# Gathers and scatters of the dense pass issued in groups of four, each group behind TensorE's next tick

## The chip, the cores and the metric

One NeuronCore of one Trainium2 chip runs the whole program. The time is the device time of one execution in microseconds (us), smaller is better. Engines are called as in the profile: PE (TensorE), DVE (VectorE), ACT (ScalarE), POOL (GpSimd) and SP (SyncE, which only issues DMAs here).

## What is computed

Four graph layers in a row on one graph of 50,000 nodes with 128 features and 25,000 edges (edges sorted by destination). Each is `x = layernorm(x + layer(x))`:

```python
# 1: two GIN convolutions and a linear layer
agg = segment_sum(x[src], dst, N); h = relu((x + agg) @ wa + ba) @ wb + bb      # per convolution
# 2: relational convolution, 8 relations, weights from 4 bases
agg = segment_sum(x[src] * edge_weight, type * N + dst); out = einsum('rni,rio->no', agg, W)
# 3: normalised graph convolution
out = segment_sum(norm * (x @ W.T)[row], col) + bias
# 4: three attention layers (softmax over the edges of a destination), each with a layer norm
```

At least half of the nodes have no incoming edge, so most of the work on the nodes needs no neighbours.

## The kernel before

Nodes are worked on as if they had no neighbours in a **dense pass** (`dense_part`), and the rows of destinations are recomputed edge by edge afterwards. The program has these stages, one behind the other: a start (weights, index columns), the dense pass together with the first edge pass of GIN (`phase_dense_gin1`), the second GIN pass, the relational pass, the normalised pass, and the three attention layers.

**Dense pass.** `DG` = 98 ticks, one per group of 512 nodes. In each tick PE, ACT, DVE and SP run stages of up to nine successive groups, tied to one another by semaphores: PE's product L856 with its semaphore `pe_a`, ACT's `de_ha` (L911), PE's L844, ACT's `de_ht` (L890), PE's transposes L849, PE's L838, ACT's `de_hh`, PE's L828 in two halves, DVE's `de_r` (L955) and the norms, PE's transposes L862 and its product L1732. A full tick has 44 matmul records on PE (a float32 matmul has two records), and the first ticks, in which the late stages have not begun, have 32. ACT's instruction at L911 runs once per tick, so its starts give the length of each tick. SP issues the loads and stores of a tick, and in the first `COPIES` = 28 ticks also one piece of 903 KB of a copy of x into the table `t_xw` (L799).

**POOL in the dense pass** runs a program of its own, `slot_gathers`, whose instructions are indirect DMAs of 128 rows each. The order is written out by hand:

- 140 gathers of destination rows of x into `msgs` (`resident_gather`, L684); 24 others went ahead in the start
- a wait until the 28 pieces of the copy have landed (`x_copied`, L705)
- 197 scatters of slot numbers, 4 bytes per row, into a column of `t_xw` (L707)
- the last 33 destination gathers (L684)
- a wait for all scatters (`mapped`), and then the gathers of source rows into a ring (L700): 16 of them at once, and each four more behind PE's and DVE's progress in the edge pass

Before the change nothing ties POOL's 370 operations to the ticks. PE waits in the first edge pass for all destination rows (`got`, L1100).

**Later edge passes** use `gather_group` (L670): four gathers per tick, with a wait for a free place in a ring of four groups ahead of each four. In the relational pass ACT's L1652 runs once per tick, in the normalised pass ACT's L1863.

Of the kernel before, what the change touches and what calls it, by code (L numbers as in the profile page):

```python
# [23 lines left out]
D = 128  # L24
# [4 lines left out]
CHUNKS = 2 * ROWP  # L29
USED = -(-E // CE)  # L30
# [3 lines left out]
DG = -(-N // GN)  # L34
# [3 lines left out]
COPIES = 28  # L38
# [4 lines left out]
UN = 4  # L43
FIRST = 24
EVERY = 5
NR = 3
XR = 6
L = 3
# [72 lines left out]
def wait(eng, sem, value):  # L121

    if not isinstance(value, int) or value > 0:
        eng.wait_ge(sem, value)
# [31 lines left out]
class Net:  # L156
# [531 lines left out]
    def slot_gathers(self, pool, ring, sem, arrived, turned, taken):  # L688


        nc, a = self.nc, self.a
        mapped = sem("g_mapped")

        def rows(i):
            u = i % UN
            if i >= UN:
                pool.wait_ge(turned, i - UN + 1)
                pool.wait_ge(taken, i - UN + 1)
            for j in self.filled(i):
                nc.gpsimd.indirect_dma_start(  # L700
                    out=ring[:, u, j, :], out_offset=None, in_=self.xw,
                    in_offset=bass.IndirectOffsetOnAxis(ap=self.src_i[:, i * G4 + j:i * G4 + j + 1], axis=0)).then_inc(arrived[u], 16)

        self.resident_gather(self.dst_i, a["x"], D, self.got, range(FIRST, FIRST + EVERY * COPIES))
        pool.wait_ge(self.x_copied, 16 * COPIES)  # L705
        for c in range(USED):
            nc.gpsimd.indirect_dma_start(  # L707
                out=self.places, out_offset=bass.IndirectOffsetOnAxis(ap=self.put_i[:, c:c + 1], axis=0),
                in_=self.slot_id[:, c:c + 1], in_offset=None).then_inc(mapped, 16)
        self.resident_gather(self.dst_i, a["x"], D, self.got, range(FIRST + EVERY * COPIES, CHUNKS))  # L710
        pool.wait_ge(mapped, 16 * USED)
        for i in range(AG):
            rows(i)
# [40 lines left out]
    def dense_part(self, block, sem, pool_program):  # L754


        nc, a = self.nc, self.a
        mem, sb, ps = self.part("de")
        with mem:
            x = sb("x", [128, UN, G4, D])  # L760
# [17 lines left out]
            s = {n: sem(n) for n in names}  # L778
            last_rows = (N - (DG - 1) * GN) // G4
            self.dense_stores = out2, out3, outx, outh  # L780

            @block.sync
            def _(sp):
# [1139 lines left out]
    def phase_gats(self):  # L1923
# [5 lines left out]
        with ctx:  # L1929
            nh = sb("nh", [128, NR, G4, XW]); nnt = sb("nnt", [D, 2, GN]); nsq = sb("nsq", [D, 2, GN])  # L1930
            nsd = sb("nsd", [128, 2, G4]); ninv = sb("ninv", [128, 2, G4])
            ah = sb("ah", [128, NR, G4, XW]); fl = sb("fl", [128, UN, GN], BF16)
            tt = sb("tt", [D, 2, GN]); ant = sb("ant", [D, 2, GN]); asq = sb("asq", [D, 2, GN])
# [10 lines left out]
            p_nh = ps("p_nh", (128, 2, 512)); p_ah = ps("p_ah", (128, 2, 512))  # L1944
            narr = [sem(f"narr{u}") for u in range(NR)]; aarr = [sem(f"aarr{u}") for u in range(NR)]; farr = [sem(f"farr{u}") for u in range(UN)]
            nout = [sem(f"nout{u}") for u in range(3)]; aout = [sem(f"aout{u}") for u in range(3)]
# [65 lines left out]
            def _(sp):  # L2012
                def nodes(i):
                    if i < NODES:
                        layer, g = divmod(i, DG)
                        wait(sp, pe_nt, i - NR + 1)
                        if layer > 0:
                            sp.wait_ge(nout[(i - DG) % 3], 16 * ((i - DG) // 3 + 1))
                        sp.dma_start(nh[:, i % NR], self.nodes(self.th[layer], 0, g)).then_inc(narr[i % NR], 16)
                    if FIRST2 <= i - 1 < NODES:  # L2020
# [14 lines left out]
                def load(layer, g):  # L2035
                    s = layer * AG + g
                    wait(sp, dve_aw, s - NR + 1)
                    if layer > 0:
# [594 lines left out]
```

## Time and profile before

| what | us |
|---|---|
| median of 3 runs | 4961.03 (4953.85 to 4983.9) |
| profiled execution | 4922.33 |
| its span | 4920.6 |

The profile covers one execution. In it the dense pass runs from about 54 us to 1185 us of the span, and the first edge pass begins its gathers again at 1232 us. Over the whole span PE is busy 62%, DVE 54%, ACT 46% and POOL 39%. Times of rows are us from the span's start; "idle before" is the time that the engine stood still ahead of a row.

### The profile page before, as it was taken

Reading aid. Unit: us, or ns where it says so; the run is one execution under the profiler, and the core shown is the slowest. Engines: PE = TensorE matmul, PEld = TensorE weight load, DVE = VectorE, ACT = ScalarE, POOL = GpSimd, SP = SyncE. Lnnn points to the kernel's source line nnn. Section 1 sums busy time; section 2 is a strip of 40 time slices with the busy share of each in tenths; the row PEclk is TensorE's granted clock in tenths of the full one; section 3 lists DMA queues with packets and bytes.
Section 4 is the critical chain, followed back from the end, with each engine's and each line's share of the span. In section 5 each row is a group of like instructions: output and inputs, shape, how many; then the busy total and the mean of one; then the engine's idle time right before and its main releaser. Section 6 shows DMA issues by size and latency. Waiting matters only on the chain. (4 is left out here: it accounts for less than half of the span.)

```text
span 4920.6 us, 67479 instructions
## 1 busy us (share of the span) xinstructions
PE 3040.0 (62%) x18099; PEld 2447.4 (50%) x18099; DVE 2637.4 (54%) x8154; ACT 2245.0 (46%) x5893; POOL 1923.9 (39%) x1994
## 2 busy tenths in 40 slices
PE   1183008997887787785664039991089991058675
PEld 1062006775443454443563039990079881057665
DVE  2083008998444565796562017770047881068876
ACT  0072008886111344675453027770057770057765
POOL 6605760000553563663664730007700007700465
PEclk8596559998776787997776569895588875586655
DMA  3293016665554343454663237772256763255443
GB/s 116 69 333 115 12 38 210 222 223 178 149 154 124 88 117 112 127 172 146 177 202 121 63 102 244 219 225 63 59 183 205 226 197 84 66 171 196 142 133 96
DMA packets 419338, 723.50 MB, mean 147 GB/s; under 512 B 76431, under 2 KB 137908, under 8 KB 418606
## 3 DMA queue, kind: packets, MB, share of 16 engines
q1 hardware_dynamic: 350990, 610.53, 38.1%
q0 software_dynamic: 63040, 107.35, 8.7%
q10 hardware_dynamic: 5024, 2.30, 0.2%
q8 instruction: 122, 2.00, 0.2%
q14 instruction: 162, 1.33, 0.1%
HBM read 428.65 MB, written 321.10 MB: 152 GB/s over the span
## 5 line engine op out<-in xcount | busy, mean ns | idle before, releaser
L684 POOL DMA_INDIRECT msgs<-t_gat,row_i x591 | 566.9, 959 | 1149.7 <-DMA t_gat<-t_hn 923.1
L1739 PE MATMUL t_p_q<-mean_col,t_nsq 128*128 128x1 f32 x2352 | 341.5, 266 | 288.7 <-issue 248.0
L1739 PEld LDWEIGHTS t_p_q<-mean_col,t_nsq 128*128 128x128 f32 x2352 | 350.7, 228 | 301.1 <-issue 301.1
L2246 ACT ACTIVATE t_nnt<-t_p_nt,cxt 128x512 f32<-128x512 f32 x294 | 200.6, 682 | 592.8 <-remote 356.8
L700 POOL DMA_INDIRECT dg_g_ring<-t_xw,src_i x197 | 189.4, 961 | 648.2 <-DVE slot_id L1203 572.6
L2083 PE MATMUL t_p_nt<-ident,t_nh 128*128 128x128 f32 x1176 | 219.5, 318 | 264.7 <-issue 179.2
L1732 PE MATMUL t_p_nh<-wx,t_nnt 128*128 128x132 f32 x1568 | 258.0, 314 | 185.8 <-issue 127.3
L2006 POOL DMA_INDIRECT out_rows<-t_hn,own_i x197 | 201.2, 1021 | 401.9 <-issue 335.3
L1732 PEld LDWEIGHTS t_p_nh<-wx,t_nnt 128*128 128x128 f32 x1568 | 222.1, 216 | 186.7 <-issue 186.1
L2083 PEld LDWEIGHTS t_p_nt<-ident,t_nh 128*128 128x128 f32 x1176 | 160.0, 164 | 280.6 <-issue 261.9
L828 PE MATMUL de_p_o<-wc,de_hh 128*128 128x128 f32 x1568 | 219.3, 284 | 112.1 <-DVE de_r L955 86.6
L1753 DVE TENSOR_TENSOR t_hn<-t_p_nh,t_ninv 128x264 f32<-128x264 f32 x392 | 151.2, 427 | 251.1 <-remote 170.1
L707 POOL DMA_INDIRECT t_xw<-slot_id,put_i x197 | 191.2, 971 | 228.2 <-DMA t_xw<-in_x_map 165.8
L828 PEld LDWEIGHTS de_p_o<-wc,de_hh 128*128 128x128 f32 x1568 | 200.8, 198 | 132.2 <-issue 113.1
L2390 DVE RECIPROCAL t_ninv<-t_nsd 128x4 f32<-128x4 f32 x196 | 34.6, 176 | 430.4 <-issue 267.3
L676 POOL DMA_INDIRECT g_ring<-t_h,row_i x197 | 193.1, 980 | 178.2 <-PE g_p_t L1344 57.0
L1732 PE MATMUL de_p_h<-wx,de_x3t 128*128 128x132 f32 x784 | 121.2, 300 | 226.5 <-issue 166.5
L676 POOL DMA_INDIRECT gc_ring<-t_x,row_i x197 | 193.3, 981 | 151.4 <-POOLq L182 57.4
L676 POOL DMA_INDIRECT rg_ring<-t_x,row_i x197 | 192.7, 978 | 149.0 <-issue 52.7
L881 ACT ACTIVATE de_hh<-de_p_c,b2a 128x512 f32<-128x512 f32 x196 | 134.9, 688 | 221.3 <-remote 217.0
L1564 PE MATMUL rg_p_b<-bases,rg_gt 128*128 128x512 f32 x400 | 205.4, 618 | 31.8 <-DVE rg_mg L1682 22.4
L1732 PEld LDWEIGHTS de_p_h<-wx,de_x3t 128*128 128x128 f32 x784 | 101.2, 199 | 248.7 <-issue 169.9
(411 smaller groups left out, 8704.4 us busy)
## 6 DMA issues: line engine op xcount, KB each, us to landing
t_gat<-t_hn SPq DMA_DIRECT2D x296, 264.0 KB
t_nh<-t_gat SPq DMA_DIRECT2D x294, 264.0 KB
t_x<-de_x SPq DMA_DIRECT2D x196, 256.0 KB
t_ah<-t_gat SPq DMA_DIRECT2D x150, 264.0 KB
t_gat<-de_h SPq DMA_DIRECT2D x98, 264.0 KB
t_xw<-in_x_map SPq DMA_DIRECT2D x28, 903.0 KB
de_xt<-in_x_t SPq DMA_DIRECT2D x98, 256.0 KB
t_xn<-t_x SPq DMA_DIRECT2D x98, 256.0 KB
```

The source lines that it names most:

```text
L676: self.nc.gpsimd.indirect_dma_start(out=ring[:, u, j, 0:width], out_offset=None, in_=table, in_offset=bass.IndirectOffsetOnAxis(ap=idx[:, ...
L684: self.nc.gpsimd.indirect_dma_start(out=self.msgs[:, c, 0:width], out_offset=None, in_=table, in_offset=bass.IndirectOffsetOnAxis(ap=idx[: ...
L700: nc.gpsimd.indirect_dma_start(out=ring[:, u, j, :], out_offset=None, in_=self.xw, in_offset=bass.IndirectOffsetOnAxis(ap=self.src_i[:, i ...
L707: nc.gpsimd.indirect_dma_start(out=self.places, out_offset=bass.IndirectOffsetOnAxis(ap=self.put_i[:, c:c + 1], axis=0), in_=self.slot_id[ ...
L828: m = nc.tensor.matmul(p_o[:, j * D:(j + 1) * D], hh[:, u % 2, t, j * D:(j + 1) * D], self.wc[:, t, :], start=(t == 0), stop=(t == 1))
L1564: nc.tensor.matmul(p_b[j][:], gt[:, (u - 1) % 2, j * D:(j + 1) * D], self.bases[:].rearrange("i b o -> i (b o)"), start=True, stop=True).t ...
L1732: last = self.nc.tensor.matmul(p_h[:, j // 2, (j % 2) * XW:(j % 2 + 1) * XW], xt[:, j * D:(j + 1) * D], self.wx[:, layer, :], start=True, ...
L1739: last = self.nc.tensor.matmul(p_q[:, j:j + 1], sq[:, j * D:(j + 1) * D], self.mean_col[:], start=True, stop=True)
L1753: last = self.nc.vector.tensor_tensor(rows[:, 2 * b:2 * b + 2, :], t, self.over(inv[:, 2 * b:2 * b + 2], XW), ALU.mult)
L2006: nc.gpsimd.indirect_dma_start(out=self.out, out_offset=bass.IndirectOffsetOnAxis(ap=self.own_i[:, c:c + 1], axis=0), in_=held[:, g % XR, ...
L2083: t = nc.tensor.transpose(p_nt[:, j * D:(j + 1) * D], nh[:, g % NR, j, 0:D], self.ident[:])
L2246: nc.scalar.activation(nnt[:, g % 2], p_nt[:], ACT.Identity, bias=bias).then_inc(act_nt, 1)
```

## The change

`slot_gathers` counts the indirect DMAs that it has issued in the dense pass. Ahead of each four (`PACE`) it waits until PE's semaphore `pe_a` has reached the number of groups issued so far plus one, so that group n goes out in tick n. The same operations are issued in the same order; the other engines' programs are not touched.

```diff
+PACE = 4
...
+        begun = self.dense_begun
+        done = [0]
+
+        def after_ticks(ops):
+            wait(pool, begun, min(done[0] // PACE + 1, DG))
+            done[0] += ops
+
+        def targets(chunks):
+            for c in range(chunks.start, min(chunks.stop, USED), PACE):
+                group = range(c, min(c + PACE, chunks.stop, USED))
+                after_ticks(len(group))
+                self.resident_gather(self.dst_i, a["x"], D, self.got, group)
...
-        self.resident_gather(self.dst_i, a["x"], D, self.got, range(FIRST, FIRST + EVERY * COPIES))
+        targets(range(FIRST, FIRST + EVERY * COPIES))
         pool.wait_ge(self.x_copied, 16 * COPIES)
         for c in range(USED):
+            if c % PACE == 0:
+                after_ticks(min(PACE, USED - c))
             nc.gpsimd.indirect_dma_start(
...
-        self.resident_gather(self.dst_i, a["x"], D, self.got, range(FIRST + EVERY * COPIES, CHUNKS))
+        targets(range(FIRST + EVERY * COPIES, CHUNKS))
...
+            self.dense_begun = s["pe_a"]
```

POOL's instructions from the start of the dense pass to the first source gathers, before:

```order
31 L813 MEMSET de_x 128x2048
32 L684 DMA msgs<-in_x,dst_i 128x128 x140
33 L707 DMA t_xw<-slot_id,put_i 6498304x1 [waits x_copied]
34 L707 DMA t_xw<-slot_id,put_i 6498304x1 x196
35 L684 DMA msgs<-in_x,dst_i 128x128 x33
36 L700 DMA dg_g_ring<-t_xw,src_i 128x129 [waits dg_g_mapped]
37 L700 DMA dg_g_ring<-t_xw,src_i 128x129 x15
```

The same place of the change, first at the step from gathers to scatters (a semaphore is printed by the first name that its number had, so `st_dst_row` stands for `pe_a`):

```order
100 L685 DMA msgs<-in_x,dst_i 128x128 [waits st_dst_row]
101 L685 DMA msgs<-in_x,dst_i 128x128 x3
102 L722 DMA t_xw<-slot_id,put_i 6498304x1 [waits st_dst_row,x_copied]
103 L722 DMA t_xw<-slot_id,put_i 6498304x1 x3
104 L722 DMA t_xw<-slot_id,put_i 6498304x1 [waits st_dst_row]
```

And at the end of the paced part:

```order
215 L685 DMA msgs<-in_x,dst_i 128x128 [waits st_dst_row]
216 L685 DMA msgs<-in_x,dst_i 128x128 x3
217 L685 DMA msgs<-in_x,dst_i 128x128 [waits st_dst_row]
218 L713 DMA dg_g_ring<-t_xw,src_i 128x129 [waits dg_g_mapped]
219 L713 DMA dg_g_ring<-t_xw,src_i 128x129 x15
```

What were three runs of 140, 197 and 33 operations with one wait among them are now 94 groups of four or fewer (35, 50 and 9), each with a wait; the last one waits for tick 93 of 98, and the sixteen source gathers follow it in one piece as they did before.

## Rows read from the trace of the kernel before

**Rows 1.** Windows: time; busy us (records) of PE, PEld, DVE, ACT, POOL; clock, DMA share, GB/s.
```profile
67.00:253.00 186.00, 24.60 (x96) 16.71 (x96) 8.79 (x35) 9.54 (x19) 123.74 (x131) 0.55 0.25 83
276.00:399.00 123.00, 111.41 (x835) 87.46 (x835) 114.09 (x455) 104.74 (x265) 0.00 (x0) 1.00 0.98 358
399.00:745.00 346.00, 39.04 (x188) 27.49 (x186) 24.41 (x99) 22.98 (x59) 240.82 (x246) 0.54 0.10 27
745.00:1168.00 423.00, 382.85 (x2854) 299.15 (x2855) 392.58 (x1562) 360.18 (x912) 0.00 (x0) 1.00 0.64 223
```

**Rows 2.** Timeline of ACT, its L911: start, us, then the instruction; once per dense tick.
```profile
66.69 0.47 ACT L911 ACTIVATE de_ha<-de_p_a,b1a 128x256 f32<-128x256 f32 x1 [1.08 <-issue]
...
252.72 0.47 ACT L911 ACTIVATE de_ha<-de_p_a,b1a 128x256 f32<-128x256 f32 x1
...
399.27 0.47 ACT L911 ACTIVATE de_ha<-de_p_a,b1a 128x256 f32<-128x256 f32 x1
...
431.12 0.47 ACT L911 ACTIVATE de_ha<-de_p_a,b1a 128x256 f32<-128x256 f32 x1 [7.47 <-issue]
...
554.32 0.47 ACT L911 ACTIVATE de_ha<-de_p_a,b1a 128x256 f32<-128x256 f32 x1 [11.73 <-remote]
...
677.52 0.47 ACT L911 ACTIVATE de_ha<-de_p_a,b1a 128x256 f32<-128x256 f32 x1 [11.74 <-remote]
...
744.97 0.46 ACT L911 ACTIVATE de_ha<-de_p_a,b1a 128x256 f32<-128x256 f32 x1
...
1174.19 0.47 ACT L911 ACTIVATE de_ha<-de_p_a,b1a 128x256 f32<-128x256 f32 x1
```

**Rows 3.** Timeline of PE in one of the long ticks.
```profile
587.35 2.05 PE L828 MATMUL de_p_o<-wc,de_hh 128*128 128x128 f32 x8 [18.91 <-DVE de_r L955]
615.13 0.66 PE L849 MATMUL de_p_b<-ident,de_ht 128*128 128x128 f32 x2 [25.73 <-issue]
```

**Rows 4.** POOL's scatters by their source line: ns min/median/max, first and last start.
```profile
L707 POOL DMA_INDIRECT t_xw<-slot_id,put_i x197: 965/970/1198, 399.4 to 652.0; - x197
```

**Rows 5.** Timeline of POOL: a destination gather, and the last source gather ahead of its pause.
```profile
231.37 0.95 POOL L684 DMA_INDIRECT msgs<-in_x,dst_i  x1 [0.30 <-issue]
...
717.00 1.09 POOL L700 DMA_INDIRECT dg_g_ring<-t_xw,src_i  x1 [0.30 <-issue]
```

**Rows 6.** Windows of the relational pass, with and without POOL's gathers.
```profile
2067.00:2097.00 30.00, 26.25 (x101) 14.71 (x100) 28.14 (x91) 23.81 (x86) 19.05 (x20) 1.00 0.62 177
2251.00:2263.00 12.00, 10.70 (x42) 6.07 (x42) 11.53 (x38) 9.79 (x36) 0.00 (x0) 1.00 0.43 136
```

**Rows 7.** ACT's L1652, once per tick of the relational pass, in the same two windows.
```profile
2067.72 0.57 ACT L1652 ACTIVATE rg_gt<-rg_p_t 128x512 f32<-128x512 f32 x1
...
2085.70 0.57 ACT L1652 ACTIVATE rg_gt<-rg_p_t 128x512 f32<-128x512 f32 x1
...
2251.75 0.57 ACT L1652 ACTIVATE rg_gt<-rg_p_t 128x512 f32<-128x512 f32 x1
...
2263.53 0.57 ACT L1652 ACTIVATE rg_gt<-rg_p_t 128x512 f32<-128x512 f32 x1
```

**Rows 8.** Normalised pass, ACT's L1863 per tick: four ticks with gathers, one without.
```profile
2406.39 0.60 ACT L1863 ACTIVATE gc_x3t<-gc_p_x 128x512 f32<-128x512 f32 x1
...
2429.98 0.58 ACT L1863 ACTIVATE gc_x3t<-gc_p_x 128x512 f32<-128x512 f32 x1
...
2615.27 0.58 ACT L1863 ACTIVATE gc_x3t<-gc_p_x 128x512 f32<-128x512 f32 x1
2619.29 0.58 ACT L1863 ACTIVATE gc_x3t<-gc_p_x 128x512 f32<-128x512 f32 x1
```

**Rows 9.** ACT's L1652 around the 28 gathers that open the relational pass.
```profile
1968.11 0.60 ACT L1652 ACTIVATE rg_gt<-rg_p_t 128x512 f32<-128x512 f32 x1
1989.83 0.57 ACT L1652 ACTIVATE rg_gt<-rg_p_t 128x512 f32<-128x512 f32 x1
```

## The prediction

> **What bounds the kernel now.** I began with the page's slices, in which PE, DVE and ACT nearly stop in two stretches of the dense pass while POOL is busy, and cut the dense pass along them [rows 1]. From 276 to 399 us, and again from 745 to 1168, POOL does nothing and PE has 6.8 records per us at full clock. From 67 to 253 and from 399 to 745 POOL issues one indirect DMA after another, and PE has 96 records in 186 us and 188 in 346 us, about 0.5 per us. It is not the DMA engines that are full: in the second such stretch they are busy 10% of the time, against 98% in the fast stretch from 276 to 399.
>
> The ticks give the price [rows 2]. From 744.97 to 1174.19 there are 66 ticks in 429.22 us, 6.50 each. From 554.32 to 677.52 one tick takes 123.20 us. The stall is in PE: its L828 has 8 records that seem to be through at 589.4 us, but the next work of PE, L849, stands until 615.13 behind 25.73 us of "issue" [rows 3]. What PE waits for there is ACT, which had itself waited for PE's earlier product; the records' ends are modelled, so PE has really not been through. 123.20 us over the 44 records of a tick is 2.80 us per record, whatever its size. POOL meanwhile issues a gather each 0.95 + 0.30 = 1.25 us and a scatter each 1.27 us [rows 4, 5], without a break. So a long unbroken run of indirect DMAs on POOL goes together with a PE that needs 2.80 us per record, and everything else in the tick hangs on PE. I can't say from the trace what PE waits for.
>
> What is lost: from 66.69 to 252.72 there are three ticks (96 records of 32 each) in 186.03 us, and from 399.27 to 744.97 four ticks in 345.70 us [rows 1, 2]. Seven ticks at 6.50 are 45.5 us; 186.03 + 345.70 - 45.5 = **486 us** lost. Since the whole program runs one stage behind the other, a dense pass that ends earlier moves everything behind it.
>
> **The change part by part.**
>
> *Removed: the long runs.* 370 operations in unbroken runs of 140 and 230 become groups of four, one per tick. If PE stays fast, a tick is 6.50 us and a group takes 4 x 1.25 = 5.0 us, at most 5.1 with scatters [rows 4, 5], so POOL keeps up and pauses at least 1.4 us per tick. Gain: 486 us, less the following.
>
> *What a group of four costs PE.* The dense pass has no such row; the nearest is the relational pass, with exactly this pattern: 20 gathers in 30 us, four per tick, at full clock [rows 6]. Its tick is (2085.70 - 2067.72) / 3 = 5.99 us with gathers and (2263.53 - 2251.75) / 2 = 5.89 without [rows 7]. That is 0.10 us per tick, with a pause of only 1 us. The lower bound is nothing: nothing in the groups helps PE. The upper bound is the normalised pass: (2429.98 - 2406.39) / 4 = 5.90 us with gathers and 4.02 without, 1.88 us more [rows 8]. Of this 0.98 is simply that four gathers take 5.0 us, which doesn't bind in a tick of 6.50; the other 0.90 could be PE's delay. The dense pass lies nearer the relational pass in its length and in the pause; but it has 44 small records with several round trips between PE and ACT in a tick, where the relational pass has 20 records and a PE that is nearly always busy. I take 0.25 us, and keep 0 and 0.9. For 65 ticks behind the copy 0.25 x 65 = 16 us.
>
> *Gathers beside the copy of x.* In the first 28 ticks the DMA engines are already busy 98% and move 358 GB/s, 2.33 MB per tick [rows 1]. Before, POOL's gathers ran there mostly while the copy crawled with the ticks. Now each of these ticks has four gathers of 128 x 512 bytes more, 0.26 MB or 11%. If the engines can't move more, a tick grows by 0.11 x 6.50 = 0.7 us; if their share has slack, by as much as any tick. I take 0.5 x 28 = 14 us (ends: 0 and 28 x 1.6 = 45, both causes at their worst).
>
> *The waits added.* POOL waits 94 times for PE's `pe_a`. Queued behind each are only POOL's own gathers and scatters. Nobody waits for these within the dense pass. The wait for `x_copied` doesn't bind any longer: the copy's last piece goes out in tick 28, and POOL gets there in tick 36. The last group goes out in tick 93, so all destination rows are there before tick 98 ends, when PE wants them. If that cover were gone (more groups than ticks), each group over would cost 5 us.
>
> *The sixteen source gathers.* They follow the last group without a break: 17 operations, 21 us, in ticks 93 to 97. The nearest row is the run of 28 gathers which opens the relational pass: the tick in it takes 1989.83 - 1968.11 = 21.72 us instead of 5.89, 16 us too many [rows 9]. This run is shorter; I take 10 us and keep 0 and 24 (up to 16, and half as much again for a tick behind it). Before, these sixteen ended at 718.1 and the tick was free again only at 744.97 [rows 2, 5], which is inside the 486.
>
> *Sum.* 486 - 16 - 14 - 10 = 446 us. Against the profiled execution 4922.3 - 446 = 4476; its time lies 38.7 under the median of the runs shown, and the same saving from the median is 4961.0 - 446 = **4515 us**. With each term at its best, 486, it is 4475; with each at its worst, 486 - 0.9 x 65 - 45 - 24 = 358, it is 4603.
>
> **The rivals.**
>
> *Partial: PE stays slow for part of every tick.* Each group of four finds 3 or 4 round trips between PE and ACT, and a delay of 2.80 us in one or two of them lengthens the tick by 2.8 to 4. For it: the normalised pass has a surplus that may be this [rows 8]. Against it: the relational pass [rows 7]. At 3 us for each of 93 ticks, 279 - 30 (what the sum has for the ticks already) = about 250 us of the gain are gone: about 4765.
>
> *No change: the cost goes by the operation.* If each indirect DMA costs PE a fixed time, 486 / 370 = 1.31 us, then spreading them out moves the cost but saves nothing: ticks of 6.5 + 5.2 = 11.7 us, the end at about 4960. For it: POOL's runs and the slow ticks coincide exactly. Against it: four gathers would cost the relational tick 5.2 us and cost it 0.10 [rows 7].
> The same time is what a rule of the Trainium skill asks for, on another mechanism: in "SBUF — State Buffer", section "SBUF: two separate sides", PE never waits for another engine's port, and DMAs and compute instructions don't slow one another. By that rule POOL's gathers are not what holds PE, and to space them out would do nothing, 4961 again. The trace speaks against the rule taken this widely: PE has 0.5 records per us beside an unbroken POOL and 6.8 without, with the DMA engines at 10% and 98%.
>
> *Slower: each group leaves PE slow beyond its own end.* After POOL's last operation at 718.1 us the next tick begins only at 744.97, 27 us later [rows 2, 5]. If a group of four already brought PE into that state, each of 94 ticks would carry such a tail. At 27 us that is 94 x 27 - 486 = 2050 us more, about 7000. It decides from 486 / 94 = 5.2 us per group on. Against it: the relational pass and, less so, the normalised one run hundreds of gathers in fours without it [rows 7, 8]. For it: only that the dense pass has shorter records and more of them.
>
> **How the numbers follow.** The forecast, with PE fast in nearly every tick: 0.86. Partial: 0.06. No change: 0.04 (0.02 by a price per operation, 0.02 by the rule of the skill's page). Slower: 0.04. The range reaches from just under the best case, 4470, to a little over the worst of the forecast's own terms, 4640, because the price of a group in a tick with many round trips is the least known of them. A change of 1% is about what a measurement of this kernel can tell from none: faster by more 0.92, within it 0.04, slower 0.04.
>
> **What would show each step.** ACT's L911 should come each 6.5 to 7.5 us from tick 3 to 93, with none over 12 us in between; ticks 4 to 28 should be somewhat longer than the later ones, with the DMA share near 1. POOL should show four operations, then an idle time of 1 us or more that ends with PE. The dense pass should end near 740 us and the source gathers begin again near 790 instead of 1232. Ticks 94 to 98 should hold one or two of 10 to 25 us. Everything behind the first edge pass should have its old length. Wrong would be: ticks near 12 us throughout (a price per operation), ticks over 12 us with PE idle behind "issue" (slow state in groups of four), or a first edge pass that begins late because POOL's last groups or its sixteen source gathers are late.

## The result, and the profile after

| | before | changed |
|---|---|---|
| median | 4972.47 us (4 runs, 4953.85 to 4987.73) | 4661.26 us (4 runs, 4620.23 to 4692.79) |
| profiled execution, its span | 4922.33, 4920.6 us | 4656.54, 4654.8 us |
| ratio of the times, 95% interval | | 0.9348 [0.9271, 0.9425] |

The change saves 311 us between the medians; the ratio leaves out the changed kernel's run of 4692.79 us, which counts as slow, being over 1.5% above the fastest. The forecast was 446, and the measured time lies 21 us above the range: the direction and the mechanism of the stall held, and one term of the sum was nine times too small.

Two of the page's rows of 40 slices, first of the kernel before, then of the changed one with its span. The two holes at the left of PE's row (dense pass) are gone, and POOL's work is spread.

```profile
PE   1183008997887787785664039991089991058675
...
POOL 6605760000553563663664730007700007700465
```

```profile
span 4654.8 us, 67480 instructions
...
PE   4877777578869968846630399930499850178665
...
POOL 5544444155365546536657300067200037400555
```

Windows of the changed kernel, in columns as in [rows 1]: the first 28 ticks (28 intervals, from the start of tick 0 to that of tick 28), the ticks with groups behind them, the last five intervals.

```profile
60.00:256.00 196.00, 161.03 (x1131) 121.04 (x1132) 149.92 (x602) 139.37 (x347) 112.50 (x113) 0.97 0.97 351
262.00:819.00 557.00, 413.35 (x2772) 313.02 (x2770) 381.76 (x1513) 350.55 (x883) 257.39 (x255) 0.93 0.52 171
819.00:873.00 54.00, 33.41 (x230) 26.55 (x229) 30.28 (x122) 28.47 (x73) 16.30 (x17) 0.81 0.44 147
```

In [rows 1] PE had 0.5 records per us while POOL worked and 6.8 while it did not. Now it has 2772 / 557 = 5.0 with POOL at work in every tick. ACT's line L911 is now L927; its starts, as in [rows 2] (tick 0, 11, 28, 36, 86, 92, 93, 94, 97):

```profile
59.83 0.47 ACT L927 ACTIVATE de_ha<-de_p_a,b1a 128x256 f32<-128x256 f32 x1 [4.26 <-PE de_p_a L872]
...
129.56 0.47 ACT L927 ACTIVATE de_ha<-de_p_a,b1a 128x256 f32<-128x256 f32 x1
...
255.73 0.47 ACT L927 ACTIVATE de_ha<-de_p_a,b1a 128x256 f32<-128x256 f32 x1
...
329.50 0.46 ACT L927 ACTIVATE de_ha<-de_p_a,b1a 128x256 f32<-128x256 f32 x1
...
768.09 0.47 ACT L927 ACTIVATE de_ha<-de_p_a,b1a 128x256 f32<-128x256 f32 x1
...
819.46 0.47 ACT L927 ACTIVATE de_ha<-de_p_a,b1a 128x256 f32<-128x256 f32 x1
844.39 0.46 ACT L927 ACTIVATE de_ha<-de_p_a,b1a 128x256 f32<-128x256 f32 x1
853.39 0.46 ACT L927 ACTIVATE de_ha<-de_p_a,b1a 128x256 f32<-128x256 f32 x1
...
872.68 0.47 ACT L927 ACTIVATE de_ha<-de_p_a,b1a 128x256 f32<-128x256 f32 x1
```

The first 28 intervals take (255.73 - 59.83) / 28 = 7.00 us each, in two parts: (129.56 - 59.83) / 11 = 6.34, then (255.73 - 129.56) / 17 = 7.42. The 50 from tick 36 to 86 take (768.09 - 329.50) / 50 = **8.77** each, where a tick without POOL takes 6.50. I use these 50 ticks as the measure for every kernel below: there each tick holds one group of four. The tick from 819.46 takes 24.93 us and the next 9.00. The last tick begins at 872.68 instead of 1174.19, 301.5 us earlier. Behind it the changed kernel takes 3782.1 us to the end of the span, the one before 3746.4.

Where a tick grew is seen in its inner order. PE, POOL and ACT of the changed kernel in one tick of 8.2 us (L860 was L844 before, L865 was L849, L906 was L890):

```profile
426.54 0.59 PE L860 MATMUL de_p_b<-de_ha,w1b 128*128 128x256 f32 x2
427.32 1.16 PE L844 MATMUL de_p_o<-wc,de_hh 128*128 128x128 f32 x8 [0.18 <-DVE de_r L971]
429.70 0.38 PE L865 MATMUL de_p_b<-ident,de_ht 128*128 128x128 f32 x2 [1.22 <-issue]
...
423.71 0.96 POOL L722 DMA_INDIRECT t_xw<-slot_id,put_i  x1 [3.03 <-PE de_p_a L872]
424.98 1.24 POOL L722 DMA_INDIRECT t_xw<-slot_id,put_i  x1 [0.30 <-issue]
...
427.80 1.04 POOL L722 DMA_INDIRECT t_xw<-slot_id,put_i  x1 [0.30 <-issue]
...
428.93 0.47 ACT L906 ACTIVATE de_ht<-de_p_b,b1b 128x256 f32<-128x256 f32 x1 [2.09 <-issue]
```

PE's L860 seems to be through at 427.13, but ACT's L906, which needs its product and nothing else at that point, begins at 428.93, after an idle time of 2.09 us, and PE then stands 1.22 us for ACT. That is [rows 3] in small: the record's modelled end is early, and the product is really there later, while POOL's four DMAs are going out. POOL's program has 3 us to spare behind PE's L872, so it is not short of time.

But the place where `de_ht` begins is telling: POOL's fourth DMA ends at 427.80 + 1.04 = 428.84, and ACT's L906 begins at 428.93. In ticks 36 to 85 of the changed kernel this is so in 46 of 50: `de_ht` begins only when the fourth DMA of the group has ended (within 0.15 us in 23, 0.6 to 1.25 us behind it in 22), although no semaphore ties it to POOL. So by the program nobody waits for POOL's groups, and yet PE's product reaches ACT only with their end.

### The profile page after: what moved, and what is told of

Its sections match the earlier page's. It is cut to its first block and busy times, and to the rows that moved or that the text cites. A ratio compares the mean times of both kernels' runs of the same rounds, so it can differ in the third digit from the quotient of the medians.

```text
span 4654.8 us, 67480 instructions
## 1 busy us (share of the span) xinstructions
PE 3064.2 (66%) x18099; PEld 2455.5 (53%) x18099; DVE 2638.3 (57%) x8154; ACT 2243.4 (48%) x5893; POOL 1936.9 (42%) x1994
## 5 line engine op out<-in xcount | busy, mean ns | idle before, releaser
L1748 PEld LDWEIGHTS t_p_nh<-wx,t_nnt 128*128 128x128 f32 x1568 | 221.5, 215 | 195.9 <-issue 195.8
L722 POOL DMA_INDIRECT t_xw<-slot_id,put_i x197 | 200.9, 1020 | 232.0 <-PE de_p_a L872 183.8
L685 POOL DMA_INDIRECT msgs<-in_x,dst_i x197 | 195.6, 993 | 173.2 <-PE de_p_a L872 116.0
L844 PE MATMUL de_p_o<-wc,de_hh 128*128 128x128 f32 x1568 | 219.1, 284 | 14.4 <-DVE de_r L971 12.4
L1580 PE MATMUL rg_p_b<-bases,rg_gt 128*128 128x512 f32 x400 | 204.3, 615 | 35.7 <-DVE rg_mg L1698 30.3
L844 PEld LDWEIGHTS de_p_o<-wc,de_hh 128*128 128x128 f32 x1568 | 203.2, 199 | 33.1 <-issue 15.2
L2268 ACT ACTIVATE t_nsd<-t_p_q,eps 128x4 f32<-128x4 f32 x294 | 77.4, 263 | 283.8 <-remote 246.4
L1343 PEld LDWEIGHTS g_p_o<-wc,g_hh 128*128 128x128 f32 x800 | 134.3, 246 | 146.1 <-issue 102.6
```

Of the source, the lines that this page charges most:

```text
L685: self.nc.gpsimd.indirect_dma_start(out=self.msgs[:, c, 0:width], out_offset=None, in_=table, in_offset=bass.IndirectOffsetOnAxis(ap=idx[: ...
L722: nc.gpsimd.indirect_dma_start(out=self.places, out_offset=bass.IndirectOffsetOnAxis(ap=self.put_i[:, c:c + 1], axis=0), in_=self.slot_id[ ...
L844: m = nc.tensor.matmul(p_o[:, j * D:(j + 1) * D], hh[:, u % 2, t, j * D:(j + 1) * D], self.wc[:, t, :], start=(t == 0), stop=(t == 1))
L1580: nc.tensor.matmul(p_b[j][:], gt[:, (u - 1) % 2, j * D:(j + 1) * D], self.bases[:].rearrange("i b o -> i (b o)"), start=True, stop=True).t ...
L1748: last = self.nc.tensor.matmul(p_h[:, j // 2, (j % 2) * XW:(j % 2 + 1) * XW], xt[:, j * D:(j + 1) * D], self.wx[:, layer, :], start=True, ...
```

## The experiments

Five groups of kernels were measured, each on one chip with its own runs of the kernel before. They are told in the order of the questions. The length of a tick is the mean over the 50 intervals of ACT's `de_ha` from tick 36 to 86, unless something else is said.

| group | kernels | before, median us (runs) |
|---|---|---|
| I | e1 to e4 | 4967.38 (1) |
| II | e5 to e8 | 4970.92 (7) |
| III | e9 to e12 | 3389.00 (13) |
| IV | f1 to f4 | 4971.08 (7) |
| V | g1, g2 | 3394.56 (19) |

e8, e12, f1, g1 and g2 have 4 to 10 runs each, the others one. The four runs of the changed kernel lie 73 us apart, so times of single runs that differ by less say little; the readings rest on the ticks of the traces, which repeat better (8.77 us in the changed kernel, 8.79 in f1, its repetition in group IV).

### Is it the group's length? Halves (e1)

```diff
-PACE = 4
+PACE = 2
...
-            wait(pool, begun, min(done[0] // PACE + 1, DG))
+            tick, half = divmod(done[0] // PACE, 2)
+            wait(pool, begun[half], min(tick + 1, DG))
...
-            self.dense_begun = s["pe_a"]
+            self.dense_begun = s["pe_a"], s["pe_b"]
```

> The changed kernel with each four cut into two groups of two, the first behind pe_a of the tick and the second behind pe_b of the next tick's start. Theory A (PE is slowed only from about 3 us after the start of a run of indirect DMAs, so that short runs are free): dense ticks of 6.5 to 7.3 us where the changed kernel has 8.0 to 9.9 between 262 and 819 us, and a time near 4530. Theory B (each operation costs PE its share, 2.1 us per four): ticks stay at 8 to 9 us and the time within 1% of 4660.

Measured: 4547.83 us, 113 less than the change. Ticks 36 and 86 of ACT:

```profile
315.71 0.46 ACT L928 ACTIVATE de_ha<-de_p_a,b1a 128x256 f32<-128x256 f32 x1
...
668.32 0.46 ACT L928 ACTIVATE de_ha<-de_p_a,b1a 128x256 f32<-128x256 f32 x1
```

(668.32 - 315.71) / 50 = 7.05 us. The same four operations per tick in two pairs cost 0.55 us instead of 2.27. So the price is not one per operation; it lies in their standing together. In none of these 50 ticks of e1 does `de_ht` begin inside one of POOL's pairs; a pair is merely over sooner.

### Whose program is held up? PE's, all four, SP's, ACT's and DVE's (e2, e3, e5, e6)

In the dense pass the programs of PE, ACT, DVE and SP are loops over four ticks (`steps`), whose waits compare a semaphore with a register. `written_out` makes the same instructions without a loop, with constants in the waits. e2 does that for PE, e3 for all four, e5 for SP, e6 for ACT and DVE; e3 is this (the others are one or two of its lines):

```diff
-                steps(sp, DG, 9, step, COPIES // UN)
+                written_out(DG, 9, step)
...
-                steps(pe, DG, 7, step, 3)
+                written_out(DG, 7, step)
...
-                steps(act, DG, 8, step, 3)
+                written_out(DG, 8, step)
...
-                steps(dve, DG, 6, step, 3)
+                written_out(DG, 6, step)
```

> The changed kernel with PE's dense program written out in all 98 ticks instead of a loop from tick 12 on. The ticks of the changed kernel grow from 6.0 to 6.6 us up to tick 10 to 7.2 and more from tick 11 on, when PE, ACT and DVE are in their loops, and to 8 to 10 when SP is too. Theory C (PE's loop, with waits against registers and its branch, is what suffers beside POOL): ticks of 6.5 to 7 us throughout, time near 4520. Theory A or B (the matmuls themselves suffer): ticks unchanged, time within 1% of 4660.

> The changed kernel with the dense programs of PE, ACT, DVE and SP all written out, no loops in the dense pass. Theory C, in the form that any engine's loop suffers beside POOL: ticks of 6.5 to 7 us from tick 11 to 93, time near 4520, also if PE's alone changed nothing. Theory A or B: unchanged, within 1% of 4660.

> The changed kernel with SP's dense program alone written out. With all four engines written out the ticks fell to 6.6 us, with PE's alone nothing changed. Theory F (SP's loop, with its waits against registers ahead of each DMA, is the partner of POOL's groups: the ticks grew again at tick 28, where SP enters its loop): ticks of 36 to 85 fall from 8.8 to about 7.3 us, the level of ticks 11 to 27, and the time to about 4570. Theory G (ACT's or DVE's loop): ticks unchanged, within 1% of 4660.

> The changed kernel with the dense programs of ACT and DVE written out, PE and SP in their loops. Theory G (ACT's or DVE's loop): ticks of 6.6 us, time near 4510. Theory F (SP's loop): ticks 11 to 27 near 6.6 us but ticks 36 to 85 still at 8 us or more, time near 4620. If loops only add up: about 7.5 us and 4580.

| kernel | written out | us | tick |
|---|---|---|---|
| the change | none | 4661.26 | 8.77 |
| e2 | PE | 4662.41 | 8.67 |
| e5 | SP | 4589.35 | 7.49 |
| e6 | ACT, DVE | 4608.94 | 7.50 |
| e3 | all four | 4507.73 | 6.72 |

Ticks 36 and 86 of e2, e5, e6 and e3, in this order:

```profile
328.54 0.46 ACT L927 ACTIVATE de_ha<-de_p_a,b1a 128x256 f32<-128x256 f32 x1
...
761.88 0.47 ACT L927 ACTIVATE de_ha<-de_p_a,b1a 128x256 f32<-128x256 f32 x1
```

```profile
321.50 0.46 ACT L927 ACTIVATE de_ha<-de_p_a,b1a 128x256 f32<-128x256 f32 x1
...
695.97 0.46 ACT L927 ACTIVATE de_ha<-de_p_a,b1a 128x256 f32<-128x256 f32 x1
```

```profile
321.42 0.46 ACT L927 ACTIVATE de_ha<-de_p_a,b1a 128x256 f32<-128x256 f32 x1
...
696.30 0.47 ACT L927 ACTIVATE de_ha<-de_p_a,b1a 128x256 f32<-128x256 f32 x1
```

```profile
304.39 0.47 ACT L927 ACTIVATE de_ha<-de_p_a,b1a 128x256 f32<-128x256 f32 x1
...
640.62 0.46 ACT L927 ACTIVATE de_ha<-de_p_a,b1a 128x256 f32<-128x256 f32 x1
```

That was the surprise of the study. PE's own loop is worth nothing (0.10 us), SP's 1.28 us and ACT's with DVE's 1.27; all four are worth 2.05 of the 2.27, somewhat less than the sum. With all four written out four indirect DMAs cost a tick 6.72 - 6.50 = 0.22 us. Against the same written-out programs beside a POOL that does nothing, 6.44 us in f4 below, it is 0.28: so 0.06 of the 2.05 us is what the loops take even without POOL. Either number is near the 0.25 that the prediction had put down.

The waits show where it goes. Columns: the engine's instruction, what it waited for, us in total, times, longest. The changed kernel from 262 to 820, e3 from 262 to 680, and the kernel before from 745 to 1168, where POOL does nothing:

```profile
ACT de_ht L906 <- remote: 150.0, 56, 5.2
```

```profile
ACT de_ht L906 <- PE de_p_b L860: 34.0, 53, 3.2
```

```profile
ACT de_ht L890 <- PE de_p_b L844: 23.9, 65, 0.5
```

ACT stands ahead of `de_ht` 2.7 us each time in the changed kernel, 0.6 in e3 and 0.4 in the kernel before. In e2, with PE's loop gone, it still stands 153.5 us in 59 times. In e3 `de_ht` no longer waits for the group's end: in 48 of 50 ticks it begins while the four DMAs are still going out. One such tick, POOL's third operation of four and ACT's `de_ht` in e3:

```profile
425.17 0.97 POOL L722 DMA_INDIRECT t_xw<-slot_id,put_i  x1 [0.31 <-issue]
...
426.05 0.47 ACT L906 ACTIVATE de_ht<-de_p_b,b1b 128x256 f32<-128x256 f32 x1 [0.56 <-PE de_p_b L860]
```

It is not that the loops have to be fetched again: from 330 to 640 us the changed kernel's instruction queues move 1 packet, e3's, without loops, 37.

The loops do not begin at once, which allows a second look inside the same traces. In all kernels the first steps of each program are written out: 12 for PE, ACT and DVE, 28 for SP. From tick 11 to 28, then, SP has no loop in any of them. The change takes 7.42 us there, e5 127.9 / 17 = 7.52 and e6 119.0 / 17 = 7.00. SP's loop is worth nothing where there is none, and 1.28 us behind it. e6 takes 0.42 less there, but this stretch repeats badly: f1, the changed kernel again, takes 7.79 in it. And up to tick 11, with groups of four but no loop at all, the change takes 6.34 (with less work in the first ticks, whose late stages have not begun).

What the loops of SP, ACT and DVE have to do with a product of PE that comes late, the trace does not show: register and branch instructions have no rows in it. Both facts stand (POOL's indirect DMAs, and other engines' loops beside them); the link between them is open.

### Is it where the group stands in the tick? (e7)

```diff
-            self.dense_begun = s["pe_a"]
+            self.dense_begun = s["pe_b"]
```

> The changed kernel with each group of four waiting for pe_b instead of pe_a, 2.5 us earlier in PE's order, all loops as they were. Theory H (what costs is that PE's L860 and L1748, on which ACT waits at once, fall into the last 2 us of a group; another place in the tick has slack): ticks of 36 to 85 fall to 7 to 7.5 us, time near 4570. Theory B (each group costs its 2.1 us wherever it stands): ticks at 8 to 9 us, time within 1% of 4660.

Measured: 4678.44 us, a tick of (783.71 - 359.38) / 50 = 8.49 us. The group of four costs nearly as much behind another of PE's products: 0.28 us per tick are gained, where e1 gained 1.72. So most of e1's gain is owed to the shorter groups, not to the place of the second.

### What about the sixteen source gathers? (e8)

e3 with the sixteen source gathers in groups of four too:

```diff
         def rows(i):
             u = i % UN
+            if i < UN:
+                after_ticks(len(self.filled(i)))
```

> All four dense programs written out, and the sixteen source gathers that follow the last group are paced as well, four in each of ticks 93 to 96. The step 'sixteen gathers cost the end of the dense pass 10 us' says: the tick of 23 to 25 us that holds 16 operations disappears, all ticks from 93 on are 6.4 to 7 us, and the time is 15 to 20 us under that with the programs written out alone, near 4490. If the long tick was owed to something else at the end of the pass, it stays and the time is within 5 us.

ACT's ticks at the end of the dense pass in e3 (where the long tick is left) and in e8:

```profile
680.11 0.47 ACT L927 ACTIVATE de_ha<-de_p_a,b1a 128x256 f32<-128x256 f32 x1
703.40 0.48 ACT L927 ACTIVATE de_ha<-de_p_a,b1a 128x256 f32<-128x256 f32 x1 [7.56 <-remote]
712.31 0.46 ACT L927 ACTIVATE de_ha<-de_p_a,b1a 128x256 f32<-128x256 f32 x1
...
731.63 0.47 ACT L927 ACTIVATE de_ha<-de_p_a,b1a 128x256 f32<-128x256 f32 x1
```

```profile
686.52 0.46 ACT L929 ACTIVATE de_ha<-de_p_a,b1a 128x256 f32<-128x256 f32 x1
...
712.54 0.47 ACT L929 ACTIVATE de_ha<-de_p_a,b1a 128x256 f32<-128x256 f32 x1
```

The tick of 23.29 us and the 8.91 behind it have gone, and the last tick begins 19.1 us earlier. Of this nothing shows in the time: 4505.39 us (4 runs, 4490.63 to 4509.05) against 4507.73 of e3's one, on another chip. From the first gather of the attention layers to the last e8's profile has 1682.4 us and e3's 1654.8, 28 less, though the code is the same in both. So the cause of the long tick is shown, and what its removal is worth is not. e8 is the fastest kernel measured in group I, II or IV, with e3 level: **0.9064 [0.9004, 0.9123]** of the kernel before, against 0.9348 of the change.

### Is it the indirect form? Memsets, plain DMAs, fewer rows (e4, f2, f3)

These start from the kernel before, without the groups. e4 leaves out the 197 scatters and has as many memsets of about the same length in their place (its later gathers read what is then in the table):

```diff
-            nc.gpsimd.indirect_dma_start(
-                out=self.places, out_offset=bass.IndirectOffsetOnAxis(ap=self.put_i[:, c:c + 1], axis=0),
-                in_=self.slot_id[:, c:c + 1], in_offset=None).then_inc(mapped, 16)
+            wait(pool, mapped, c)
+            nc.gpsimd.memset(ring[:].rearrange("p a b c -> p (a b c)")[:, 0:1024], 0.0).then_inc(mapped, 1)
...
-        pool.wait_ge(mapped, 16 * USED)
+        pool.wait_ge(mapped, USED)
```

> The kernel before (no pacing), with its 197 scatters replaced by 197 memsets of 128x1024 float32 on POOL, each behind the last one's end. Part of the computation is left out: the slot numbers are not written, so later passes read other rows. Theory D (indirect DMAs are what slows PE): during the memsets the dense ticks are 6.5 us and the time is near 4961 - 320 = 4640. Theory E (a busy POOL of any kind slows PE): ticks of 123 us during the memsets, time near 4960.

```profile
401.00:598.00 197.00, 173.66 (x1271) 132.34 (x1271) 186.80 (x690) 159.81 (x405) 185.55 (x195) 1.00 0.62 216
```

POOL is busy 94% of this window with 195 memsets, and PE has 1271 / 197 = 6.5 records per us, against 0.5 beside the scatters [rows 1]. A POOL that is busy with memsets holds nobody up. e4 took 4727.83 us, 88 more than its expectation had for this case: the 49 indirect DMAs that follow the memsets without a pause bring ticks of 23.5 and 51.4 us, and the part behind the last tick takes 3798 us.

f2 replaces the 140 gathers by plain DMAs of 128 x 512 bytes, without indices (so other rows arrive than are wanted):

```diff
-        self.resident_gather(self.dst_i, a["x"], D, self.got, range(FIRST, FIRST + EVERY * COPIES))
+        for c in range(FIRST, FIRST + EVERY * COPIES):
+            nc.gpsimd.dma_start(self.msgs[:, c, 0:D], a["x"][c * 128:(c + 1) * 128, :]).then_inc(self.got, 16)
```

> The kernel before with 140 plain DMAs of 128 rows of 512 bytes from POOL in place of its first 140 destination gathers (left out: the right rows of those chunks), again, on what may be a chip with the stall. Theory D1 (any DMA whose descriptors POOL writes slows PE): long ticks near 90 us between 67 and 253 us, about 4960. Theory D2 (only the indirect form): ticks of 6.5 us there, near 4800. On a chip without the stall both give about 3390.

Its windows, with the plain DMAs beside the copy of x, and later with the unchanged scatters, and the plain DMAs by their source line:

```profile
67.00:138.00 71.00, 57.66 (x372) 42.87 (x372) 47.84 (x196) 44.85 (x107) 63.08 (x120) 0.91 1.03 385
279.00:525.00 246.00, 21.00 (x88) 14.49 (x88) 12.18 (x48) 11.25 (x28) 185.04 (x192) 0.52 0.08 19
```

```profile
L705 POOL DMA_DIRECT2D msgs<-in_x x140: 542/663/837, 55.9 to 137.6; - x140
```

140 DMAs issued by POOL without a pause leave PE at 5.2 records per us, with the DMA engines full; the same place had 0.5 in [rows 1]. In the same execution the indirect scatters then bring ticks of 123.2 us again. So it is neither that POOL issues DMAs nor their traffic, but the indirect form. f2 took 4826.99 us. The Trainium skill ("SBUF — State Buffer", section "SBUF: two separate sides") says that DMAs don't slow compute instructions; for the plain DMAs this trace agrees, for the indirect ones of groups I, II and IV it does not.

f3 lets each scatter write 32 rows instead of 128 (three quarters of the slot numbers are left out):

```diff
-                out=self.places, out_offset=bass.IndirectOffsetOnAxis(ap=self.put_i[:, c:c + 1], axis=0),
-                in_=self.slot_id[:, c:c + 1], in_offset=None).then_inc(mapped, 16)
+                out=self.places, out_offset=bass.IndirectOffsetOnAxis(ap=self.put_i[0:32, c:c + 1], axis=0),
+                in_=self.slot_id[0:32, c:c + 1], in_offset=None).then_inc(mapped, 16)
```

> The kernel before with 32 of 128 rows in each of its 197 scatters (left out: three quarters of the slot numbers), again. Theory R (each row's descriptor costs PE): the ticks of 123.2 us fall in proportion, to 30 us or so. Theory O (it is the operation): they stay at 123.2 us. On a chip without the stall about 3385.

```profile
L707 POOL DMA_INDIRECT t_xw<-slot_id,put_i x197: 856/865/1821, 399.3 to 647.1; - x197
```

```profile
587.21 0.47 ACT L911 ACTIVATE de_ha<-de_p_a,b1a 128x256 f32<-128x256 f32 x1 [11.73 <-remote]
...
710.40 0.47 ACT L911 ACTIVATE de_ha<-de_p_a,b1a 128x256 f32<-128x256 f32 x1 [11.73 <-remote]
```

A quarter of the rows takes POOL 0.865 us instead of 0.970 [rows 4], and the tick is 123.19 us long, as with all rows. So the rows don't matter. Nor does each operation have a price: f3's two full slow ticks hold 98 and 89 operations of POOL, those of the kernel before 95 and 98, and all four take 123.2 us. What is constant is the 2.80 us per record of PE; a slow tick of the kernel before in its first stretch, with 32 records, takes 89.60 us (tick 2), which is 2.80 again. f3 took 4946.95 us.

### Are the loops alone to blame? (f4)

f4 is the kernel before, without groups, with all four programs written out as in e3.

> The kernel before, unpaced, with its four dense programs written out, again. Theory S (loops only decide what a short group costs): ticks of 123 us remain, about 4960. Theory L (loops are the cause): ticks under 15 us, about 4520. On a chip without the stall about 3370.

```profile
539.34 0.47 ACT L911 ACTIVATE de_ha<-de_p_a,b1a 128x256 f32<-128x256 f32 x1 [11.03 <-remote]
...
662.56 0.47 ACT L911 ACTIVATE de_ha<-de_p_a,b1a 128x256 f32<-128x256 f32 x1 [11.03 <-issue]
```

A tick of 123.22 us, 4973.76 us in all: nothing is gained. From tick 36 to 86, where POOL does nothing, a tick takes 6.44 us (322.0 / 50), against 6.50 with the loops. Without pauses of POOL the loops don't matter, and with pauses they are most of what is left. In the long runs PE's records keep their 2.80 us whatever the engines' programs look like.

### The change once more (f1)

> The changed kernel once more, since the last four kernels met a chip on which the kernel before takes 3389 us and shows no long ticks. On such a chip: nothing to win, within 1% of the kernel before, ticks of 6.4 to 7.2 us in both. On a chip where the kernel before takes about 4960 us: ratio 0.935 to 0.94 again, ticks of 8.8 us from 36 to 85.

The changed kernel in group IV: 4653.38 us (4 runs, 4627.69 to 4665.16), ratio 0.9355 [0.9307, 0.9403], a tick of 8.79. The part behind its last tick takes 3767 us.

### Two groups in which there was no stall (e9 to e12, g1, g2)

f2, f3 and f4 had run before, as e9, e10 and e11, with e12: halves as in e1, all programs written out, and the sixteen source gathers in pairs.

> The kernel before (unpaced), with its first 140 destination gathers replaced by 140 plain DMAs from POOL of the same size, 128 rows of 512 bytes with a fixed address. Left out of the computation: the right destination rows of those chunks. Theory D1 (any DMA whose descriptors POOL writes slows PE): the long ticks between 67 and 253 us stay, near 90 us each, and the time is near 4960. Theory D2 (only the indirect form does): ticks of 6.5 us there, and about 165 us less, near 4800.

> The kernel before (unpaced), with its 197 scatters reduced to 32 of the 128 rows each. Left out: three quarters of the slot numbers, so later passes read other rows. Theory R (each row's descriptor costs PE): the ticks of 123.2 us during the scatters fall in proportion, to 30 us or so. Theory O (it is the operation): as long as they follow one another without a pause the ticks stay at 123.2 us, only for a shorter time if one operation takes less than its 1.27 us.

> The kernel before (no pacing), with the dense programs of PE, ACT, DVE and SP written out. Theory S (the loops only decide how much a short group costs; in an unbroken run PE is slow anyway, as in the first ticks, which were never in a loop): ticks of about 123 us remain, time near 4960. Theory L (loops are the true cause and pacing is not needed): ticks under 15 us throughout, time near 4520.

> All four dense programs written out, groups of two (behind pe_a and behind pe_b), and the sixteen source gathers paced in the same way. Theory T (what is left of the group's price, 6.58 us against 6.50, and the tick of 8 to 11 us here and there go with groups of two): ticks of 6.5 us, 5 to 10 us under the 4505 us of the kernel with groups of four. If more waits cost POOL or PE anything: ticks near 6.7 to 7 us, 4515 to 4550.

They told nothing of what was asked, since in this group the kernel before took 3389.0 us (13 runs, 3378.39 to 3398.42) and not 4970. e9 took 3396.31, e10 3381.01, e11 3366.51 and e12 3375.15 us, ratio 0.9961 [0.9940, 0.9982]. e11 has POOL's long runs untouched:

```profile
60.00:678.00 618.00, 554.65 (x4145) 438.98 (x4146) 555.42 (x2254) 515.23 (x1308) 371.01 (x378) 1.00 0.80 279
```

```profile
240.50 0.48 ACT L911 ACTIVATE de_ha<-de_p_a,b1a 128x256 f32<-128x256 f32 x1
246.94 0.47 ACT L911 ACTIVATE de_ha<-de_p_a,b1a 128x256 f32<-128x256 f32 x1
```

The tick beside POOL's unbroken scatters is 6.44 us. The same instructions in the same order that stop PE in f4 cost it nothing here. Whole executions of the kernel before are 1580 us shorter in this group, far more than the 486 us of the dense pass. Behind the last tick e11 takes 3364.7 - 678.4 = 2686 us, the kernel before in [rows 2] 4920.6 - 1174.2 = 3746. The change leaves that part alone, and its trace shows one place: each of the three attention layers has POOL issue 197 gathers in one run. Windows of the same length from the start of the first of these runs, of the changed kernel and of e11:

```profile
2365.00:2612.00 247.00, 32.83 (x135) 28.60 (x135) 11.08 (x35) 10.17 (x19) 187.03 (x195) 0.50 0.26 70
```

```profile
1897.00:2144.00 247.00, 231.45 (x1924) 225.96 (x1925) 162.17 (x474) 170.49 (x398) 187.07 (x196) 0.93 0.87 274
```

With the stall PE has 135 records in 247 us, 0.55 per us, as in the first row of [rows 1]; without it 1924, beside as many gathers. So the attention layers hold a larger loss of the same kind. Whether groups would help there too was not tried.

g1 (e12 again) and g2 (e8 again) were to be compared with each other:

> Four dense programs written out, groups of two (behind pe_a and pe_b), the sixteen source gathers paced too, again, and beside its sister with groups of four on one chip. Theory T: on a chip with the stall ticks of 6.5 us where groups of four have 6.6 to 6.7, 5 to 15 us less. If the place of the delay in the tick matters more than its size: up to 7.1 us per tick, as groups of two had with the loops, and 4530 to 4550. On a chip without the stall about 3375, and no difference.

> The same with groups of four: on a chip with the stall 4505 us again, ratio 0.906 to the kernel before, ticks of 6.6 to 6.7 us. On a chip without the stall about 3375.

The kernel before took 3394.56 us there (19 runs), so this group had no stall either. g1 took 3378.49 us, ratio 0.9949 [0.9923, 0.9975], and g2 3382.88, ratio 0.9958 [0.9931, 0.9986]: both gain half a per cent, and their ticks are 6.43. Whether pairs beat fours when all programs are written out was not measured where the stall is.

Within a group either all runs had the stall or none. Groups IV and V, though, carry the same number of the chip, some minutes apart, the one with the stall and the other without. So whether it belongs to a chip or to a condition that a chip is in, the runs leave open.

## Why the prediction was off

**What bounds the kernel: right.** The long ticks went with POOL's unbroken runs, and in groups of four they are gone. e4 and f2 show what the prediction could not tell: it takes indirect DMAs. f3 shows that the number of rows doesn't matter. What it takes besides, groups III and V leave open: there the same runs stop nobody.

**Removed, 486 us: right**, as the seven long ticks no longer stand anywhere in the trace.

**What a group of four costs PE, 16 us: wrong, and this is the miss.** Taken were 0.25 us per tick, with 0.9 as the worst. From tick 28 to tick 92 there are 64 intervals in 819.46 - 255.73 = 563.7 us, 8.81 each; over 6.50 that is 2.31 x 64 = 148 us, 132 more than the term. Ticks of 6.5 to 7.5 us had been named as the sign; and the source gathers begin again at 928 us instead of near 790. The step that failed was the choice of the nearest row for this term. The prediction weighed the relational and the normalised pass by their records and pauses, and overlooked that the engines' programs in both are written out, while those of the dense pass are loops (`steps`, L870, L928, L993 and L807 of the kernel before). e3 takes the loops away and finds 0.22 us per tick (0.28 against f4), between the 0.10 of [rows 7] and the 0.90 of [rows 8]: the rows fit programs of the form that they came from. An upper bound from a stage whose programs have another form was no bound.

**Gathers beside the copy, 14 us: right in size, for another reason.** The first 28 intervals take 195.9 us, and the forecast was 28 x 6.50 + 14 = 196. But the 11 before the loops take 6.34 us, with the DMA share at 0.97 over all 28, and the 17 behind, with three of the loops begun, 7.42, which e3 without loops cuts to 6.65. So part of what was put down to the copy comes from the loops; how much is left for it I can't say. That the term came out right is luck.

**The waits added: right for the program, not for the chip.** POOL stands 3.03 us behind PE's L872 in the tick shown, and no semaphore waits for its groups. But ACT's `de_ht` begins behind the group's end in 46 of 50 ticks, which the prediction did not foresee.

**The sixteen source gathers, 10 us: half of what they cost.** The five intervals from 819.46 to 872.68 take 53.2 us, 20.7 more than 5 x 6.50, inside the 0 to 24 that were kept. e8 shows that these gathers are the cause.

**The sum.** 446 were forecast to be gone by the last tick, and 301.5 were. 132 and 11 us of the two terms are the 144 that are missing.

**That everything behind the first edge pass has its old length: not quite.** Behind the last tick the changed kernel took 35.7 us longer. The largest piece is the second GIN pass, 392 us against 372. I don't count it to the change: f4, whose program behind the dense pass is that of before, takes 3801.0 us behind its last tick and not 3746.4, and its second GIN pass is as long as that of the changed kernel (347.1 and 347.9 us from the first gather to the last, 326.9 in the kernel before). The profiled execution of before was simply a quick one, 50 us under its median, so that the saving between medians, 311 us, is nearer to the 301.5 of the dense pass than to the 265.8 between the two profiles.

**The rivals.** "Partial" is what happened in kind, though not as told: a tick has a delay of about 2.3 us instead of 2.8 to 4, and it hangs on the programs' form. "No change", by a price per operation, is refuted for groups of four: it asked for 5.2 us per tick, and four operations cost 2.27 us in one group, 0.55 in two pairs and 0.22 to 0.28 beside programs without loops. The rule of the Trainium skill's page would have had the spacing do nothing, which is wrong where the stall is; in groups III and V it is nearly right. The spaced kernels gain half a per cent there, and e11, written out and not spaced, has 3366.51 us, as little as any of them. "Slower" didn't happen: the longest tick beside a group of four is 13.3 us in the changed kernel and 14.4 in f1.

## To carry to other kernels

Where PE nearly stops beside an engine that issues indirect DMAs without a pause, give that engine a pause in every tick, in the smallest groups that keep up; pairs were cheaper than fours (0.55 against 2.27 us per tick). When a cost is borrowed from another stage, compare the form of the programs too (loops with register waits or written out), not only the tile sizes and the busy shares: here it made the cost nine times the term. And when the effect is a stall whose cause is unknown, measure before and after on the same chip at the same time, since the same program took 4970 us in three groups and 3390 in two.

## What was not expected of the hardware

- A stall that is there or not for one and the same program, by 1580 us of 4970, with POOL's gathers of equal length in both (0.94 to 0.95 us).
- In it, a matmul record of PE costs 2.80 us beside a run of indirect DMAs of POOL, whether these have 128 or 32 rows, and beside memsets or plain DMAs of POOL it does not. The price goes by PE's records: a tick takes 123.2 us with 89 operations of POOL in it as with 98.
- Beside groups of four, and with the loops, ACT's `de_ht`, which needs a product of PE, begins only when the group is over (46 of 50 ticks); with all programs written out it begins in the middle of the group (48 of 50).
- The loop of SP, which computes nothing, is worth 1.28 us of a tick of 8.77 beside POOL's groups, and those of ACT and DVE 1.27; PE's own is worth 0.10.
- What PE waits for in all this has no row in the trace. The modelled ends of its records hide it, and only the engine that needs the product shows it (ACT's L906: 2.09 us).
